# A GNN kernel: the seats' rows of sweep A and of the last layer through two row buffers instead of one

## The chip, the cores and the metric

The kernel runs on one core of one Trainium2 chip. The metric is the device time of one launch in microseconds (us), as the median of several runs. Besides, one execution was recorded by the hardware profiler; every row below is from that execution.

## The reference, cut to what matters

There are 100,000 nodes with 64 features each, and 50,000 edges with their own 64 features, sorted by destination. Four layers are added to `x` one after the other, each on the normalised rows `h = max(layernorm(x), 0)`:

```python
h = jnp.maximum(_layernorm(x, axis=-1), 0.0)
x = x + _L0_gnn_ref(h, edge_index, W3, b3, W4, b4)      # two graph convolutions: sweeps A and B
h = jnp.maximum(_layernorm(x, axis=-1), 0.0)
x = x + _L1_gnn_ref(h, edge_index, edge_attr_64, W, b, eps)   # edge features: sweep C
h = jnp.maximum(_layernorm(x, axis=-1), 0.0)
x = x + _L2_gnn_ref(h, attn_w, temp, src, dst)          # 8 attention steps: layer D
h = jnp.maximum(_layernorm(x, axis=-1), 0.0)
x = x + _L3_gnn_ref(h, src, dst)                        # 10 propagation steps: layer E, the last
```

A step of a layer sums, for each destination, rows gathered from its sources. In `_L0_gnn_ref` the rows are scaled by `dinv`, the inverse root of the degree; in `_L3_gnn_ref` the result of the 10 steps is mixed as `out = out + w[step + 1] * h`, beginning with `w[0] * feat`.

## The kernel before, in words

**Seats and chunks.** Each edge has a seat: partition `p`, column `j`, with 392 columns on 128 partitions. The columns are worked on in `NCH = 28` chunks of `CH = 14`. One chunk of rows is a tile of 128 x 14 x 64 floats, 448 KB. `X` holds the state of the destination at each seat in SBUF, with two more columns (`FC` and the next) for the segments that reach over partitions; these two columns are the "tail" below.

**Tables.** For each sweep a table in HBM (`tab_a` to `tab_e`) holds the rows that are gathered: first those of all nodes, then from row N those of the seats. The nodes' part is written in the dense stage, the first third of the run, in which each tile passes through two row buffers in turn: `row_ac = [rowsA, rowsC]` and `row_be = [rowsB, rowsE]`. The seats' part is written by a pass over the chunks just ahead of each sweep, or within the sweep before.

**The two passes that the change touches.** For sweep A and for layer E nothing is swept while the seats' rows are made, so each has a pass of its own, of 28 iterations.

- VectorE (DVE): wait until the row buffer's last store has landed (`stored["a"]`, `stored["e"]`), then `norm`: 14 `bn_stats` (L1253), a few short operations on the statistics, `sem_inc(var_ready)`, the centred rows `xm` (L1265), wait for the square root of ScalarE, the reciprocal (L1267), the scaled rows into the row buffer (L1269). Pass A then scales them by `dinv` (L1292), pass E adds them to `X` (L1366). Then `sem_inc(rows_ready)` (L1368 in pass E). Pass A first copies the chunk of `dinv` (L1710). Pass A is stage_a with `rowsA` at L1708 to L1714, pass E is stage_e with `rowsE` at L2072 to L2076.
- ScalarE (ACT): `root` (the square root, L735), then `store_rows` (L764): wait for `rows_ready`, issue one DMA of the whole chunk to the table.
- After the 28 chunks comes the tail of two columns, in the same row buffer, and its first column is scattered to the table by GpSimd (POOL) in `front_rows` (L450). Only then, and when all stores have landed, does POOL begin the gathers of the sweep.

**What runs beside them.** In pass A, POOL works off `attr_rows`: for each of 28 chunks it gathers 14 columns of the edge features (L446) into `G` and stores them to `attr` in two halves (L570). POOL comes to `front_rows(tab_a, ...)` after the last of these. In pass E, POOL has nothing to do: the attention steps are over, and the last layer's first gather needs `tab_e`. SyncE (SP) waits on `stored["a"]` (L412) and `f_stored` (L414) before it loads the chunks of `tab_a` for sweep A.

**Order.** Every engine runs its program in order, with loops written out by hand; there is no planner. A register (`Reached`) holds the value of a semaphore that an engine waits for next. `fresh()` clears `dve_step`, on which DVE waits for its own earlier results, once in each loop iteration.

Of the kernel before, what the change touches and what calls it, by code (L numbers as in the profile page):

```python
# [3 lines left out]
def _build(nc, x, src, dst, edge_attr, W3, b3, W4, b4, W1, b1, eps, attn_w, temp, out):  # L4
# [22 lines left out]
    FC = COLS  # L27
    XC = COLS + 2
# [19 lines left out]
    with ctx:  # L48
# [3 lines left out]
        def sem(name):  # L52
            return ctx.enter_context(nc.semaphore(name))
# [4 lines left out]
        tab_a = dram("tab_a", [N + EP, D])  # L58
# [3 lines left out]
        tab_e = dram("tab_e", [N + REG, D])  # L62
# [11 lines left out]
        X = sb("X", [P, XC, D])  # L74
# [16 lines left out]
        dinv = sb("dinv", [P, XC])  # L91
# [40 lines left out]
        mixb = sb("mixb", [P, K3 + 1])  # L132
# [24 lines left out]
        rowsA = sb("rowsA", [P, CH, D])  # L157
# [50 lines left out]
        row_ac = [rowsA, rowsC]  # L208
        row_be = [rowsB, rowsE]
# [13 lines left out]
        dve_step = sem("dve_step")  # L223
# [37 lines left out]
        x_free = [sem("x_free0"), sem("x_free1")]  # L261
        out_stored = [sem("out_stored0"), sem("out_stored1")]
        rows_ready = sem("rows_ready")
        stored = {k: sem(f"stored_{k}") for k in "abcde"}
        dense_stored = {k: [sem(f"dense_{k}0"), sem(f"dense_{k}1")] for k in "abcde"}
        var_ready = sem("var_ready")
        sd_ready = sem("sd_ready")
# [12 lines left out]
        f_rows = sem("f_rows")  # L280
# [24 lines left out]
        FIRST = 1  # L305
# [15 lines left out]
        def wide(t, n=D):  # L321

            return t.unsqueeze(2).to_broadcast([t.shape[0], t.shape[1], n])
# [16 lines left out]
        def _(sp):  # L340
# [62 lines left out]
            sp.wait_ge(widest_stored, 16)  # L403
            sp.dma_start(WB[:, 2:7], widest.rearrange("a o -> o a").to_broadcast([P, 5])).then_inc(widest_loaded, 16)
            r_fs = Reached(sp, "sp_fs")
            r_st = {k: Reached(sp, f"sp_stored_{k}", FIRST) for k in "abc"}
            for k, t in (("a", tab_a), ("b", tab_b), ("c", tab_c)):
                if k == "c":
                    sp.wait_ge(attr_stored[0], 16 * NCH)
                    sp.wait_ge(attr_stored[1], 16 * NCH)  # L410
                sp.wait_ge(stored[k], r_st[k].more(16 * NCH))
                sp.sem_inc(sp_waited, 1)  # L412
                sp.wait_ge(f_stored, r_fs.more(16))
                sp.sem_inc(sp_waited, 1)  # L414
                with sp.Fori(0, NCH // 2) as i:
                    for s in (0, 1):
                        c = 2 * i + s
                        sp.wait_ge(used[s], r_used[s].reg)
                        sp.sem_inc(sp_waited, 1)
                        r_used[s].skip(1)  # L420
                        sp.dma_start(own[:, s, :, :], seats(t, N, c)).then_inc(own_loaded[s], 16)
                        if k == "c":
                            sp.dma_start(ea[:, s, :, :], seats(attr, 0, c)).then_inc(ea_loaded[s], 16)

        @block.gpsimd
        def _(pool):
# [203 lines left out]
                pool.wait_ge(f_stored, r_fs.more(16))  # L630
                pool.sem_inc(pool_waited, 1)

            r_stored = {k: Reached(pool, f"pool_stored_{k}", FIRST) for k in "abcde"}
            front_rows(tab_a, F_TAB_W, fown[:, 0, :])
            pool.wait_ge(stored["a"], r_stored["a"].more(16 * NCH))
            pool.sem_inc(pool_waited, 1)
            pool.wait_ge(dense_stored["a"][0], FIRST + 16 * NT // 2)
            pool.wait_ge(dense_stored["a"][1], FIRST + 16 * NT // 2)
# [34 lines left out]
                    pool.wait_ge(step_done, r_sd.more(1))  # L673
                    pool.sem_inc(pool_waited, 1)
            front_rows(tab_e, F_TAB_W, rowsE[:, 0, :])
            pool.wait_ge(stored["e"], r_stored["e"].more(16 * NCH))
            pool.sem_inc(pool_waited, 1)
            pool.wait_ge(dense_stored["e"][0], FIRST + 16 * NT // 2)
            pool.wait_ge(dense_stored["e"][1], FIRST + 16 * NT // 2)
# [45 lines left out]
        def _(act):  # L725
# [48 lines left out]
            for s in (0, 1):  # L774
                act.sem_inc(raw_stored[s], FIRST)
                act.sem_inc(out_stored[s], FIRST)
                for k in "abcde":
                    act.sem_inc(dense_stored[k][s], FIRST)
            for k in "abcde":
                act.sem_inc(stored[k], FIRST)  # L780

            r_be = [Reached(act, f"act_be{s}", FIRST) for s in (0, 1)]
# [76 lines left out]
            act.wait_ge(var_ready, r_var.more(1))  # L859
            nc.scalar.activation(tmpB[:, :], snE[:, :], ACT.Sqrt).then_inc(sd_ready, 1)  # L860

            with act.Fori(0, NCH) as c:
                root(CH)
                store_rows(seats(tab_a, N, c), rowsA[:, :, :], stored["a"])
            root(2)

            def raw_and_hidden(c, s, before=None):
# [55 lines left out]
            with act.Fori(0, NCH) as c:  # L923
                root(CH)
                store_rows(seats(tab_e, N, c), rowsE[:, :, :], stored["e"])
            root(2)

            def step_e(table, first, k):
# [160 lines left out]
        def _(dve):  # L1089
# [5 lines left out]
            r_stored = {k: Reached(dve, f"dve_st_{k}", FIRST) for k in "abcde"}  # L1095
# [12 lines left out]
            def nth():  # L1108

                steps[0] += 1  # L1110
                return steps[0]
# [160 lines left out]
            def xcols(c):  # L1272
                return X[:, ds(c * CH, CH), :]
# [16 lines left out]
            def stage_a(xr, dv, R, ready):  # L1290
                norm(xr, rowsA[:, 0:R, :], R)
                v.tensor_tensor(rowsA[:, 0:R, :], rowsA[:, 0:R, :], wide(dv), ALU.mult).then_inc(dve_step, 1)  # L1292
                dve.wait_ge(dve_step, nth())
                dve.sem_inc(ready, 1)

# [64 lines left out]
                attention_row(rowsD[:, 0:R, :], xr, R)  # L1360
                dve.sem_inc(ready, 1)

            def stage_e(xr, R, ready):

                norm(xr, rowsE[:, 0:R, :], R)
                v.scalar_tensor_tensor(xr, rowsE[:, 0:R, :], mixb[:, 0:1], xr, ALU.mult, ALU.add).then_inc(dve_step, 1)  # L1366
                dve.wait_ge(dve_step, nth())
                dve.sem_inc(ready, 1)  # L1368

# [335 lines left out]
            dve.wait_ge(dve_step, nth())  # L1705

            dve.wait_ge(x_gathered, 16 * (COLS + 1))
            with dve.Fori(0, NCH) as c:  # L1708
                fresh()
                v.tensor_copy(chn[:, 0, :], dinv[:, ds(c * CH, CH)]).then_inc(dve_step, 1)  # L1710
                dve.wait_ge(dve_step, nth())
                dve.wait_ge(stored["a"], r_stored["a"].reg)
                r_stored["a"].skip(16)
                stage_a(xcols(c), chn[:, 0, :], CH, rows_ready)  # L1714
            dve.wait_ge(stored["a"], r_stored["a"].reg)
            stage_a(X[:, FC:XC, :], dinv[:, FC:XC], 2, f_rows)
# [352 lines left out]
            with dve.Fori(1, K2 + 1) as k:  # L2069
                fresh()  # L2070
                step_d(k)
            with dve.Fori(0, NCH) as c:  # L2072
                fresh()
                dve.wait_ge(stored["e"], r_stored["e"].reg)
                r_stored["e"].skip(16)
                stage_e(xcols(c), CH, rows_ready)  # L2076
            dve.wait_ge(stored["e"], r_stored["e"].reg)
            v.tensor_copy(idxC[:, :], idxA[:, :]).then_inc(dve_step, 1)
            dve.wait_ge(dve_step, nth())
            stage_e(X[:, FC:XC, :], 2, f_ready)  # L2080
            dve.wait_ge(f_stored, r_fs.more(16))
            begin()

# [81 lines left out]
```

## Time and profile before

| | us |
|---|---|
| median of 3 runs | 9849.85 |
| lowest and highest run | 9848.82 and 9856.18 |
| profiled execution, its own time | 9845.43 |
| its span | 9843.8 |
| DVE busy | 5536.8 (56%) |
| POOL busy | 6361.7 (65%) |
| ACT busy | 593.6 (6%) |
| PE busy (matmul) | 1625.2 (17%) |

The span is the time from the first to the last recorded instruction. An engine's share of busy time is a mean over stages that differ: dense stage, sweeps A to C, attention steps, last layer. The end of the run is set by whichever engine is last in each stage, so a pass is judged by its own stretch: pass A lies between about 3426 and 3693 us, pass E between about 7402 and 7664 us.

### The profile page before, as it was taken

The page shows a single profiled execution, that of the slowest core. Times are in us where ns is not written, and L with a number is a line of the kernel's source. Part 1 is how long each engine was busy: PE and PEld are TensorE (multiplying, and loading weights), DVE is VectorE, ACT ScalarE, POOL GpSimd, SP SyncE. Part 2 cuts the span into 40 slices and gives each one's busy share as a digit, 9 for nine tenths or more (in the row PEclk, how much of TensorE's full clock was granted, in tenths as well). Part 3 has the DMA queues.
Part 4 walks back from the last instruction along what each step waited for, and adds up shares of the span by engine and source line. Part 5 has one row for each costly group of instructions (what it writes and reads, how often), then busy time and mean ns, then how long its engine had stood idle before and what let it go on. Part 6 is the DMA issues. An engine that isn't in the chain of part 4 may idle for free.

```text
span 9843.8 us, 60633 instructions
## 1 busy us (share of the span) xinstructions
PE 1625.2 (17%) x7434; PEld 1157.5 (12%) x7434; DVE 5536.8 (56%) x16716; ACT 593.6 (6%) x1219; POOL 6361.7 (65%) x6415
## 2 busy tenths in 40 slices
PE   5634231210244302540012200000000000000000
PEld 1223131110233201430011100000000000000000
DVE  6769484683999861436678845545446443333310
ACT  0011010000111100110000000000001000000000
POOL 6767755527477777767767577666640677777777
PEclk9855555555555555555555555555555555555555
DMA  0022120100234432333333322242221121333320
GB/s 10 11 80 95 49 78 31 52 28 0 71 114 124 115 88 67 91 84 90 91 93 100 86 45 50 43 42 39 37 27 45 43 47 40 44 42 39 35 26 19
DMA packets 588778, 568.96 MB, mean 58 GB/s; under 512 B 420588, under 2 KB 426657, under 8 KB 588624
## 3 DMA queue, kind: packets, MB, share of 16 engines
q0 software_dynamic: 193184, 160.50, 12.3%
q10 hardware_dynamic: 368192, 328.20, 10.0%
q1 hardware_dynamic: 27346, 79.76, 2.4%
q14 instruction: 51, 0.42, 0.0%
q8 instruction: 5, 0.08, 0.0%
HBM read 214.35 MB, written 357.51 MB: 58 GB/s over the span
## 4 chain that ended last, share of the span: by engine, by line
POOL 44%; issue 24%; DVE 19%; DMA 11%; POOLq 1%; DVEq 1%; PE 0%; SPq 0%; ACTq 0%; ACT 0%
POOL G L446 23%; POOL look L446 5%; DVE G L1740 5%; POOL X L446 4%; POOL pair L446 4%; POOL seatmap L450 4%; POOL out L450 3%; DMA G<-in_edge_attr,idxs 1%; DVE st L1253 1%; DMA G<-tab_d,idxs 1%; DMA alt_d<-G 1%; DMA G<-alt_d,idxs 1%; DMA tab_e<-rowsE 1%; DVE xm L1278 1%; DVE G L1989 1%
## 5 line engine op out<-in xcount | busy, mean ns | idle before, releaser
L446 POOL DMA_INDIRECT G<-tab_e,idxs x644 | 681.7, 1058 | 230.3 <-issue 188.8
L446 POOL DMA_INDIRECT G<-tab_d,idxs x616 | 640.2, 1039 | 221.2 <-issue 176.6
L446 POOL DMA_INDIRECT look<-flagtab,idxs x588 | 614.9, 1046 | 206.8 <-issue 170.2
L2118 DVE TENSOR_TENSOR G<-G,chn 128x896 f32<-128x896 f32 x76 | 83.2, 1095 | 938.8 <-DMA G<-tab_e,idxs 548.0
L446 POOL DMA_INDIRECT X<-in_x,dst_gat x392 | 421.1, 1074 | 249.1 <-issue 125.8
L446 POOL DMA_INDIRECT G<-alt_e,idxs x420 | 444.7, 1059 | 154.7 <-issue 127.6
L446 POOL DMA_INDIRECT G<-tab_c,idxs x392 | 441.9, 1127 | 142.9 <-issue 117.7
L974 PE MATMUL TR<-w4T,shared 128*128 128x64 f32 x2356 | 488.7, 402 | 190.2 <-ACT shared L753 190.2
L446 POOL DMA_INDIRECT G<-tab_b,idxs x392 | 419.2, 1069 | 141.1 <-issue 113.5
L446 POOL DMA_INDIRECT pair<-lookup,idxs x392 | 418.5, 1068 | 140.3 <-issue 116.5
L974 PEld LDWEIGHTS TR<-w4T,shared 128*128 128x128 f32 x2356 | 475.4, 312 | 283.5 <-issue 283.5
L446 POOL DMA_INDIRECT G<-in_edge_attr,idxs x392 | 413.1, 1054 | 140.9 <-issue 129.8
L446 POOL DMA_INDIRECT G<-alt_d,idxs x392 | 408.2, 1041 | 140.6 <-issue 113.7
L450 POOL DMA_INDIRECT seatmap<-vals,idxs x392 | 399.5, 1019 | 140.8 <-issue 116.5
L446 POOL DMA_INDIRECT G<-tab_a,idxs x392 | 395.4, 1009 | 141.4 <-issue 110.8
L991 PE MATMUL HP<-ident,tcar 128*64 128x128 f32 (+1 forms) x21 | 8.7, 416 | 2694.5 <-DVEq L1189 2694.5
L1253 DVE BATCH_NORM_STATS2 st<-xin 128x6 f32<-128x64 f32 x3136 | 419.1, 210 | 57.9 <-DVE rowsC L1269 17.1
L984 PE MATMUL TR<-w1Te,hT 64*128 64x64 f32 x1568 | 182.1, 420 | 1188.5 <-ACT hT L743 1188.5
L1964 DVE RECIPROCAL sm<-G 128x14 f32<-128x14 f32 x72 | 17.4, 242 | 617.8 <-DMA G<-tab_d,idxs 361.3
L1740 DVE SCALAR_TENSOR_TENSOR G<-G,chn 128x64 f32<-128x64 f32 x1092 | 311.6, 285 | 39.1
L966 PE MATMUL HP<-hT,w3T 64*128 64x512 f32 (+1 forms) x676 | 282.0, 982 | 235.3 <-ACT hT L743 235.3
L991 PEld LDWEIGHTS HP<-ident,tcar 128*64 128x64 f32 (+1 forms) x21 | 3.2, 150 | 2698.6 <-issue 2698.6
(465 smaller groups left out, 7530.5 us busy)
## 6 DMA issues: line engine op xcount, KB each, us to landing
raw<-G ACTq DMA_DIRECT2D x84, 448.0 KB, 3.6
tab_d<-rowsD ACTq DMA_DIRECT2D x56, 469.0 KB, 2.6
tab_d<-G ACTq DMA_DIRECT2D x56, 469.0 KB, 2.8
xin<-in_x SPq DMA_DIRECT2D x56, 448.0 KB, 5.6
tab_a<-rowsA ACTq DMA_DIRECT2D x56, 448.0 KB, 2.5
tab_b<-rowsB ACTq DMA_DIRECT2D x56, 448.0 KB, 2.8
out<-shared ACTq DMA_DIRECT2D x56, 448.0 KB, 5.6
tab_c<-rowsC ACTq DMA_DIRECT2D x56, 448.0 KB, 2.6
```

What stands on the lines that cost most here:

```text
L446: pool.indirect_dma_start(to, None, table, bass.IndirectOffsetOnAxis(ap=index, axis=0), bounds_check=bound, oob_is_err=False).then_inc(s, 16)
L450: pool.indirect_dma_start(table, bass.IndirectOffsetOnAxis(ap=index, axis=0), frm, None, bounds_check=bound, oob_is_err=False).then_inc(s, 16)
L966: last = nc.tensor.matmul(HP[:, 2 * h + g, 0:(b - a) * P], w3T[h * D:(h + 1) * D, :], hT[h * D:(h + 1) * D, a:b, :].rearrange("p a b -> p ...
L974: last = nc.tensor.matmul(T[:, r * D:(r + 1) * D], U[:, r % 2, r // 2, :], w4T[:, :], start=True, stop=True)
L984: last = nc.tensor.matmul(T[:, at:at + D], hT[h * D:(h + 1) * D, r // 2, :], w[h * D:(h + 1) * D, :], start=True, stop=True)
L991: nc.tensor.transpose(to, frm, ident[0:n, 0:n]).then_inc(turned, 1)
L1253: last = v.bn_stats(st[:, r, :], xr[:, r, :])
L1278: v.tensor_tensor(xm[:, 0:R, :], to[:, :, 0:D], flat_rows(attn[:, k * D:(k + 1) * D], R), ALU.mult).then_inc(dve_step, 1)
L1740: v.scalar_tensor_tensor(G[:, s, j, 0:W], before, go[:, j:j + 1], G[:, s, j, 0:W], ALU.mult, ALU.add).then_inc(dve_step, 1)
L1964: v.reciprocal(r1, g[:, :, D + 2]).then_inc(dve_step, 1)
L1989: v.tensor_tensor(g, g, wide(p, AW), ALU.mult).then_inc(dve_step, 1)
L2118: v.tensor_tensor(g, g, wide(chn[:, 1, :]), ALU.mult).then_inc(dve_step, 1)
```

## The change

Both passes now go two chunks to an iteration, `s = 0` and `s = 1`, and 14 iterations. Chunk `2i + s` goes through `row_ac[s]` (pass A: `rowsA`, `rowsC`) or `row_be[s]` (pass E: `rowsB`, `rowsE`). Each buffer has a store semaphore of its own, `seats_stored[k][s]`, in place of the one `stored[k]`; whoever waited for all 28 stores now waits on both, with 14 each. The tail of pass A stays in `rowsA` and waits on the stores of buffer 0; the tail of pass E stays in `rowsE` and waits on those of buffer 1.

```diff
-        stored = {k: sem(f"stored_{k}") for k in "abcde"}
+        stored = {k: sem(f"stored_{k}") for k in "bcd"}
+        seats_stored = {k: [sem(f"seats_{k}0"), sem(f"seats_{k}1")] for k in "ae"}
...
-                sp.wait_ge(stored[k], r_st[k].more(16 * NCH))
+                if k == "a":
+                    sp.wait_ge(seats_stored["a"][0], FIRST + 16 * NCH // 2)
+                    sp.wait_ge(seats_stored["a"][1], FIRST + 16 * NCH // 2)
+                else:
+                    sp.wait_ge(stored[k], r_st[k].more(16 * NCH))
...
-            pool.wait_ge(stored["a"], r_stored["a"].more(16 * NCH))
+            pool.wait_ge(seats_stored["a"][0], FIRST + 16 * NCH // 2)
+            pool.wait_ge(seats_stored["a"][1], FIRST + 16 * NCH // 2)
... (the same for "e")
-            with act.Fori(0, NCH) as c:
-                root(CH)
-                store_rows(seats(tab_a, N, c), rowsA[:, :, :], stored["a"])
+            with act.Fori(0, NCH // 2) as i:
+                for s in (0, 1):
+                    root(CH)
+                    store_rows(seats(tab_a, N, 2 * i + s), row_ac[s][:, :, :], seats_stored["a"][s])
... (the same for "e", with row_be)
-            with dve.Fori(0, NCH) as c:
+            with dve.Fori(0, NCH // 2) as i:
                 fresh()
-                v.tensor_copy(chn[:, 0, :], dinv[:, ds(c * CH, CH)]).then_inc(dve_step, 1)
-                dve.wait_ge(dve_step, nth())
-                dve.wait_ge(stored["a"], r_stored["a"].reg)
-                r_stored["a"].skip(16)
-                stage_a(xcols(c), chn[:, 0, :], CH, rows_ready)
-            dve.wait_ge(stored["a"], r_stored["a"].reg)
-            stage_a(X[:, FC:XC, :], dinv[:, FC:XC], 2, f_rows)
+                for s in (0, 1):
+                    c = 2 * i + s
+                    v.tensor_copy(chn[:, 0, :], dinv[:, ds(c * CH, CH)]).then_inc(dve_step, 1)
+                    dve.wait_ge(dve_step, nth())
+                    dve.wait_ge(seats_stored["a"][s], r_seats["a"][s].reg)
+                    r_seats["a"][s].skip(16)
+                    stage_a(row_ac[s][:, :, :], xcols(c), chn[:, 0, :], CH, rows_ready)
+            dve.wait_ge(seats_stored["a"][0], r_seats["a"][0].reg)
+            stage_a(rowsA[:, 0:2, :], X[:, FC:XC, :], dinv[:, FC:XC], 2, f_rows)
...
-            with dve.Fori(0, NCH) as c:
+            with dve.Fori(0, NCH // 2) as i:
                 fresh()
-                dve.wait_ge(stored["e"], r_stored["e"].reg)
-                r_stored["e"].skip(16)
-                stage_e(xcols(c), CH, rows_ready)
-            dve.wait_ge(stored["e"], r_stored["e"].reg)
+                for s in (0, 1):
+                    dve.wait_ge(seats_stored["e"][s], r_seats["e"][s].reg)
+                    r_seats["e"][s].skip(16)
+                    stage_e(row_be[s][:, :, :], xcols(2 * i + s), CH, rows_ready)
+            dve.wait_ge(seats_stored["e"][1], r_seats["e"][1].reg)
             v.tensor_copy(idxC[:, :], idxA[:, :]).then_inc(dve_step, 1)
             dve.wait_ge(dve_step, nth())
-            stage_e(X[:, FC:XC, :], 2, f_ready)
+            stage_e(rowsE[:, 0:2, :], X[:, FC:XC, :], 2, f_ready)
```

`stage_a` and `stage_e` take the buffer as their first argument, and their operations stay the same ones.

## Rows read from the trace of the kernel before

**Rows 1.** The page, its chain that ended last, by engine.

```profile
POOL 44%; issue 24%; DVE 19%; DMA 11%; POOLq 1%; DVEq 1%; PE 0%; SPq 0%; ACTq 0%; ACT 0%
```

**Rows 2.** POOL's waits, 7664 to 9500: line, releaser, us, times, longest us.

```profile
POOL tab_e L450 <- DVEq L1368: 268.2, 1, 268.2
```

**Rows 3.** DVE's waits in pass E, 7401.6 to 7664.

```profile
DVE st L1253 <- DMA tab_e<-rowsE: 76.7, 27, 2.9
DVE idxC L2078 <- DMA tab_e<-rowsE: 2.7, 1, 2.7
```

**Rows 4.** Timeline, first chunks of pass E: start, duration, what, [idle before <- releaser].

```profile
7402.22 1.87 DVE L1253 BATCH_NORM_STATS2 st<-X 128x6 f32 x14 [0.68 <-DVE eidx L1923]
...
7407.46 1.15 DVE L1366 SCALAR_TENSOR_TENSOR X<-rowsE,mixb,X 128x896 f32 x1
7408.86 0.34 ACTq L764 DMA_DIRECT2D tab_e<-rowsE  x1
7409.53 1.28 ACT L735 ACT_TABLE_LOAD   x1 [4.23 <-DVEq L1368]
7411.46 1.87 DVE L1253 BATCH_NORM_STATS2 st<-X 128x6 f32 x14 [2.85 <-DMA tab_e<-rowsE]
...
7414.25 0.31 ACT L735 ACTIVATE lnw<-lnw,lneps 128x14 f32<-128x14 f32 x1 [3.43 <-DVEq L1264]
```

**Rows 5.** Chain that ended last, a piece of pass E: start, us, what.

```profile
7408.86 2.44 DMA tab_e<-rowsE
```

**Rows 6.** Timeline of DVE in layer E: between chunks, at a loop's end and inside its body.

```profile
7798.39 0.17 DVE L2113 COPY chn<-cont 128x14 f32 x1 [0.78 <-DVE X L2124]
...
7817.78 0.17 DVE L2113 COPY chn<-cont 128x14 f32 x1 [0.26 <-DVE X L2124]
```

**Rows 7.** DVE's waits in pass A, 3426 to 3693.

```profile
DVE st L1253 <- DMA tab_a<-rowsA: 59.4, 28, 3.0
DVE chn L1710 <- DVE rowsA L1292: 18.0, 27, 0.7
```

**Rows 8.** DVE's waits in the dense stage, 500 to 3380.

```profile
DVE st L1253 <- DVE rowsC L1269: 16.6, 20, 0.9
DVE st L1253 <- DVE rowsA L1269: 10.3, 27, 0.4
```

**Rows 9.** One line of the code: DVE's waits on semaphores within stage_a, min/median/max ns.

```profile
L1294 DVEq EVENT_SEMAPHORE  x29: 21/21/21, 3433.2 to 3692.3; - x29
```

**Rows 10.** Timeline of ACT in layer D: table loads of two successive loop iterations.

```profile
5714.30 1.28 ACT L772 ACT_TABLE_LOAD   x1 [7.39 <-issue]
5753.39 1.28 ACT L772 ACT_TABLE_LOAD   x1 [7.35 <-issue]
```

**Rows 11.** Timeline, end of pass A.

```profile
3692.36 0.23 DVE L1717 COPY fown<-rowsA 128x128 f32<-128x128 f32 x1
```

**Rows 12.** Timeline of POOL: heads of attr chunks in and after pass A, then front_rows.

```profile
3453.47 0.21 POOL L557 COPY idxs<-eidx 128x14 int32 x1
...
3688.70 0.21 POOL L557 COPY idxs<-eidx 128x14 int32 x1
...
3711.19 0.21 POOL L557 COPY idxs<-eidx 128x14 int32 x1
...
3778.86 0.21 POOL L557 COPY idxs<-eidx 128x14 int32 x1
3798.19 0.98 POOL L570 DMA_DIRECT2D attr<-G  x1
3804.98 1.07 POOL L450 DMA_INDIRECT tab_a<-fown,fidx  x1 [3.50 <-issue]
```

**Rows 13.** SP's waits, 3300 to 3900.

```profile
SPq L412 <- DMA tab_a<-rowsA: 265.7, 1, 265.7
SPq L414 <- DMA tab_a<-fown,fidx: 117.2, 1, 117.2
```

**Rows 14.** The tile attr: time from issue to landing of its DMAs.

```profile
DMA to landing us min/median/max: 3.1/3.1/6.9
```

More of the change, by code:

```diff
@@ L405, in _ @@
             r_fs = Reached(sp, "sp_fs")
-            r_st = {k: Reached(sp, f"sp_stored_{k}", FIRST) for k in "abc"}
+            r_st = {k: Reached(sp, f"sp_stored_{k}", FIRST) for k in "bc"}
             for k, t in (("a", tab_a), ("b", tab_b), ("c", tab_c)):
@@ L631, in front_rows @@
                 pool.sem_inc(pool_waited, 1)
-            r_stored = {k: Reached(pool, f"pool_stored_{k}", FIRST) for k in "abcde"}
+            r_stored = {k: Reached(pool, f"pool_stored_{k}", FIRST) for k in "bcd"}
             front_rows(tab_a, F_TAB_W, fown[:, 0, :])
-            pool.wait_ge(stored["a"], r_stored["a"].more(16 * NCH))
+            pool.wait_ge(seats_stored["a"][0], FIRST + 16 * NCH // 2)
+            pool.wait_ge(seats_stored["a"][1], FIRST + 16 * NCH // 2)
             pool.sem_inc(pool_waited, 1)
@@ L675, in _ @@
             front_rows(tab_e, F_TAB_W, rowsE[:, 0, :])
-            pool.wait_ge(stored["e"], r_stored["e"].more(16 * NCH))
+            pool.wait_ge(seats_stored["e"][0], FIRST + 16 * NCH // 2)
+            pool.wait_ge(seats_stored["e"][1], FIRST + 16 * NCH // 2)
             pool.sem_inc(pool_waited, 1)
@@ L778, in _ @@
                     act.sem_inc(dense_stored[k][s], FIRST)
-            for k in "abcde":
+                for k in "ae":
+                    act.sem_inc(seats_stored[k][s], FIRST)
+            for k in "bcd":
                 act.sem_inc(stored[k], FIRST)
@@ L922, in _ @@
                 step_d(tab_d, N, 2 * n + 2)
-            with act.Fori(0, NCH) as c:
-                root(CH)
-                store_rows(seats(tab_e, N, c), rowsE[:, :, :], stored["e"])
+            with act.Fori(0, NCH // 2) as i:
+                for s in (0, 1):
+                    root(CH)
+                    store_rows(seats(tab_e, N, 2 * i + s), row_be[s][:, :, :], seats_stored["e"][s])
             root(2)
@@ L1094, in _ @@
             r_turned = Reached(dve, "dve_turned")
-            r_stored = {k: Reached(dve, f"dve_st_{k}", FIRST) for k in "abcde"}
+            r_stored = {k: Reached(dve, f"dve_st_{k}", FIRST) for k in "bcd"}
+            r_seats = {k: [Reached(dve, f"dve_seats_{k}{s}", FIRST) for s in (0, 1)] for k in "ae"}
             r_gat = [Reached(dve, f"dve_gat{s}") for s in (0, 1)]
@@ L1288, in attention_row, with stage_a @@
                 dve.wait_ge(dve_step, nth())
-            def stage_a(xr, dv, R, ready):
-                norm(xr, rowsA[:, 0:R, :], R)
-                v.tensor_tensor(rowsA[:, 0:R, :], rowsA[:, 0:R, :], wide(dv), ALU.mult).then_inc(dve_step, 1)
+            def stage_a(to, xr, dv, R, ready):
+                norm(xr, to, R)
+                v.tensor_tensor(to, to, wide(dv), ALU.mult).then_inc(dve_step, 1)
                 dve.wait_ge(dve_step, nth())
@@ L1361, in stage_d, with stage_e @@
                 dve.sem_inc(ready, 1)
-            def stage_e(xr, R, ready):
-                norm(xr, rowsE[:, 0:R, :], R)
-                v.scalar_tensor_tensor(xr, rowsE[:, 0:R, :], mixb[:, 0:1], xr, ALU.mult, ALU.add).then_inc(dve_step, 1)
+            def stage_e(to, xr, R, ready):
+                norm(xr, to, R)
+                v.scalar_tensor_tensor(xr, to, mixb[:, 0:1], xr, ALU.mult, ALU.add).then_inc(dve_step, 1)
                 dve.wait_ge(dve_step, nth())
@@ L2071, in _ @@
                 step_d(k)
-            with dve.Fori(0, NCH) as c:
+            with dve.Fori(0, NCH // 2) as i:
                 fresh()
-                dve.wait_ge(stored["e"], r_stored["e"].reg)
-                r_stored["e"].skip(16)
-                stage_e(xcols(c), CH, rows_ready)
-            dve.wait_ge(stored["e"], r_stored["e"].reg)
+                for s in (0, 1):
+                    dve.wait_ge(seats_stored["e"][s], r_seats["e"][s].reg)
+                    r_seats["e"][s].skip(16)
+                    stage_e(row_be[s][:, :, :], xcols(2 * i + s), CH, rows_ready)
+            dve.wait_ge(seats_stored["e"][1], r_seats["e"][1].reg)
             v.tensor_copy(idxC[:, :], idxA[:, :]).then_inc(dve_step, 1)
             dve.wait_ge(dve_step, nth())
-            stage_e(X[:, FC:XC, :], 2, f_ready)
+            stage_e(rowsE[:, 0:2, :], X[:, FC:XC, :], 2, f_ready)
             dve.wait_ge(f_stored, r_fs.more(16))
```

## The prediction

> **What bounds the kernel now.** I read the chain that ended last first. POOL has 44% of it, DVE 19%, DMA 11% [rows 1]: mostly the run waits for POOL's gathers, but there are stages in which DVE and a DMA are last. So the two passes have to be looked at one by one, and the question for each is who waits for whom at its end.
>
> Pass E is on the path. POOL sits idle for 268.2 us until DVE's `sem_inc` after the tail (L1368) [rows 2]; the pass with its tail takes the whole of that. Within it DVE waits 27 times, 76.7 us in total, for the store of the chunk before to land [rows 3]: 2.84 us each. The order in a chunk is strict [rows 4]: the last operation on the rows ends at 7407.46 + 1.15 = 7408.61, ACT issues the store at 7408.86, it takes 2.44 us to land [rows 5], and only then, at 7411.46, does the next `bn_stats` start, which doesn't touch the row buffer at all. From the first `bn_stats` to the end of L1366 DVE needs 7408.61 - 7402.22 = 6.39 us, so the period of 9.24 us is 6.39 of work and 2.85 of waiting.
>
> Pass A is not on the path. It looks alike: 59.4 us of waits for the store (28 times, the last of them the tail's), and 18.0 us of gaps at the loop's end [rows 7]. But its tail is over at 3692.6 [rows 11], while POOL is still at the edge features: the head of its last chunk is at 3778.86, the store of its first half is issued at 3798.19, and `front_rows` of `tab_a` comes at 3804.98 [rows 12]. DVE's result lies ready for 112 us. SP says the same: 117.2 us in its wait for that scatter, after the wait for pass A [rows 13].
>
> **The change part by part.**
>
> *Pass E, the waits removed.* Chunk c now waits for the store of chunk c-2. That store is issued 0.25 us after the end of its chunk and lands 2.44 us later, at +2.69 us; DVE asks for the buffer one chunk and two gaps later, 6.39 + 0.3 + 0.75 = +7.4 us. A landing would have to take 7.1 us to be felt. So all 27 waits go: -76.7 us.
>
> *Pass E, what was hidden beneath these waits.* Between two chunks DVE still has to signal `rows_ready`, add to a register, look at a semaphore, compute the address of the next chunk, and at the loop's end branch and clear `dve_step`. This has been free under the DMA, and now shows. The trace has the same pair of gaps in layer E's loop, also two chunks to a body: 0.78 us at the loop's end and 0.26 us inside the body [rows 6]. Pass A's own loop end is 18.0 / 27 = 0.67 us [rows 7]. In the dense stage, two waits and two register additions ahead of the `bn_stats` give 10.3 / 27 = 0.38 inside the body and 16.6 / 20 = 0.83, longest 0.9, at the loop's end [rows 8]. One more wait than in rows 6 is 0.02 us [rows 9]. I take 0.30 inside the body (bounds 0.26 and 0.38) and 0.75 at the loop's end (bounds 0.67 and 0.9), near rows 6 since that is the closest code. There are 14 steps from s = 0 to s = 1 and 13 back: 14 x 0.30 + 13 x 0.75 = 4.2 + 9.75 = 13.95 us. With the bounds, 14 x 0.26 + 13 x 0.67 = 12.3 and 14 x 0.38 + 13 x 0.9 = 17.0.
>
> *Pass E, next in line: ACT.* Its square root must be ready. After the store's issue ACT loads its function table from 7409.53 to 7410.81, that is 2.20 us after the end of L1366 [rows 4]. The square root itself is called for 7414.25 - 7411.46 = 2.79 us after `bn_stats` starts. With gaps of 0.30 and 0.75 that is at +3.1 and +3.5, so 0.9 and 1.3 us are left: nothing is late. If that cover were too short it would cost the difference per chunk. Besides, a loop with two chunks to a body needs one load in each iteration, as in layer D, where they are 39.1 us apart [rows 10], so I expect 13 or 14 loads instead of 27.
>
> The Trainium skill counts more for this load: in "ScalarE: Activation LUTs", section "What ACT_TABLE_LOAD costs", about 1283 ns and then a drain of about 1380 ns, 2.66 us in all. The first figure is that of rows 4; a drain no row here shows, since no activation follows a load closely. By that page ACT would be free at +3.58 us: 0.04 us late after a loop's end, 0.5 us late inside the body if there is a load there too, so an estimate of 0.5 us in total with one load per iteration, 7 us with one per chunk.
>
> *Pass E, the tail.* The last chunk used `rowsE`, the tail does too, and it waits for that store: the 2.7 us of L2078 [rows 3] stay. POOL's and SP's second wait are on semaphores that are long reached, 0.02 us each [rows 9].
>
> Pass E: -76.7 + 13.95 = -62.7 us, bounds -64.4 and -59.7. POOL's first gather of layer E starts by so much earlier, and after that nothing is changed: POOL bounds the ten steps as before.
>
> *Pass A.* The same arithmetic makes it some 60 us shorter, and all of it goes into waiting: SP waits for `front_rows` for some 177 us instead of 117, POOL doesn't look. 0 us. The tail of pass A has no wait any more, since buffer 0 is free by then; 0 as well.
>
> *Pass A, beside POOL.* Here may be a small effect of unknown sign. From 3453.47 to 3688.70 POOL needs 235.23 / 10 = 23.52 us a chunk, from 3711.19 to 3778.86 only 67.67 / 3 = 22.56 [rows 12]. So pass A costs POOL, which is on the path, 0.96 us a chunk, some 11 us over its 266 us. If this is tied to the work of DVE and the 28 stores, which stay the same in number, nothing changes. If it is tied to the time in which both run, a pass shorter by 60 us gives 0.96 x 60 / 23.5 = 2.5 us back. If denser stores collide more, the most I allow is that the excess doubles: 11 us lost. I take 0, between the two and near the first, as the work is what collides.
>
> **Sum.** -62.7 us. The profiled execution took 9845.43, its span 9843.8, so I expect 9782.7 and 9781.1 there. It stood 4.4 below the median of the runs; from the median, 9849.85 - 62.7 = 9787.1. I predict 9787.
>
> **The rivals.**
>
> 1. *Pass A, denser, slows POOL.* For: the 0.96 us a chunk above; the stores then come every 7 us instead of every 9.3. Against: no more bytes or operations, and POOL has only some nine chunks under pass A instead of eleven. 9787 + 11 = 9798.
>
> 2. *A new wait in pass E takes the place of the old*, on ACT's square root or in a store that lands late beside the next chunk's operations. For: DVE and the store now overlap fully, which in this pass has not been. Against: the slack of 0.9 us and more worked out above, and the dense stage, which overlaps in the same way with gaps of 0.4 and 0.8 [rows 8]. If half of each wait stayed, 27 x 1.42 = 38.3 with the gaps within it, the gain is 38 us: 9812.
>
> 3. *The pass isn't what holds POOL.* If something else would end its wait just as late, the time stays 9850. For: only that sweep A shows how it goes, with 112 us of cover [rows 11, 12]. Against: in pass E POOL has no work, and its wait ends with DVE's signal [rows 2].
>
> 4. *Slower: the doubled loop bodies.* A body twice as long might have to be fetched again at each jump back. The longest landing of a DMA in the attr stores is 6.9 us [rows 14]; 13 such stalls in pass E are 90 us, less the 62.7 gained, 9877. It decides from 62.7 / 13 = 4.8 us a jump; at the 2.44 us of a store the result would still be 31 us faster. Against: the dense loop's body has some 196 DVE operations, pass E's would have 46, and the dense loop turns back in 0.83 us, 0.9 at the most [rows 8]. The Trainium skill has the mechanism ("Runtime: NRT & Kernel Launch", section "Instruction fetch mechanics"): a taken branch outside the two-page window has to fetch its target first. Rows 8 show no trace of it at four times the length.
>
> **How the numbers follow.** Forecast 0.85; rival 1 0.06; rival 2 0.06; rival 3 0.02; rival 4 0.01. The forecast's own bounds are 9785.5 (gaps at their lowest) to 9790.1; with 2.5 us back from pass A 9783, with a part of rival 1 about 9795. The runs before lay between 9848.8 and 9856.2, and the profiled one at 9845.4, so the level itself moves by 4 to 6 us either way. The range is 9777 to 9801, which takes in rival 1. About 0.2%, 20 us, is what a measurement of this kernel can tell from no change. Forecast, rival 1 and rival 2 are all faster by more than that: 0.97. Same 0.02, slower 0.01.
>
> **What would show it.** In the changed profile: no wait of `bn_stats` for a DMA in pass E, but gaps of about 0.3 and 0.75 us in turn; a pair of chunks in 2 x 6.39 + 1.05 = 13.8 us; POOL's wait at L450 down from 268.2 to about 205 us; the tail's wait still 2.7; ACT's table loads in pass E 13 or 14. Pass A over near 3632 us and SP's wait at L414's place near 177, with POOL's scatter of `fown` within 3 us of 3805. I would be wrong if POOL's wait in pass E fell by clearly less than 60 us, if that scatter moved by more than 5 us, or if the layers after pass E took longer than before.

## The result, and the profile after

| | before | after |
|---|---|---|
| median (8 runs each, same chip) | 9848.61 | 9814.67 |
| lowest and highest run | 9839.02 and 9856.18 | 9806.85 and 9832.76 |
| profiled execution, its own time | 9845.43 | 9815.84 |
| its span | 9843.8 | 9814.2 |
| pass E: last scatter of layer D to first of layer E | 269.3 | 209.2 |
| eight attention steps | 1737.0 | 1747.9 |
| ten steps of the last layer | 1823.7 | 1837.6 |

The ratio is 0.9968, with a 95% interval of 0.9957 to 0.9979: 33.9 us faster, where 62.7 were forecast, and outside the range given. The stages in the table are measured between POOL's `fidx` scatters, as in [rows 12].

Pass E does what it should. These are DVE's waits in it, the view of [rows 3] (line and tile, releaser, us in total, times, longest us):

```profile
DVE st L1265 <- DVE X L1378: 14.9, 27, 0.9
DVE idxC L2093 <- DMA tab_e<-rowsE: 2.7, 1, 2.7
```

The 76.7 us of waiting for a store are gone. In their place are 14.9 us of gaps, where 13.95 were forecast, and the tail's 2.7 stay. In the timeline of DVE, as in [rows 4 and 6], the two gaps follow each other (start, duration, what, idle before):

```profile
7424.21 1.15 DVE L1378 SCALAR_TENSOR_TENSOR X<-rowsB,mixb,X 128x896 f32 x1
7425.67 1.87 DVE L1265 BATCH_NORM_STATS2 st<-X 128x6 f32 x14 [0.31 <-DVE X L1378]
...
7430.92 1.15 DVE L1378 SCALAR_TENSOR_TENSOR X<-rowsE,mixb,X 128x896 f32 x1
7432.94 1.95 DVE L1265 BATCH_NORM_STATS2 st<-X 128x6 f32 x14 [0.86 <-DVE X L1378]
...
7438.27 1.15 DVE L1378 SCALAR_TENSOR_TENSOR X<-rowsB,mixb,X 128x896 f32 x1
```

A pair of chunks takes 7438.27 - 7424.21 = 14.06 us; 13.8 were forecast. The third line holds a detail for later: the 14 `bn_stats` of `s = 0` take 1.95 us, those of `s = 1` 1.87. ACT is on time. Its groups in pass E show 13 table loads, where the kernel before had 27, and its timeline shows the square root called 2.86 us after the start of the `bn_stats` at 7432.94, the load long over:

```profile
L742 ACT ACT_TABLE_LOAD x13 | 16.7, 1283 | 54.9 <-DVEq L1380 54.9
```
```profile
7433.00 1.28 ACT L742 ACT_TABLE_LOAD   x1 [4.24 <-DVEq L1380]
7435.80 0.31 ACT L742 ACTIVATE lnw<-lnw,lneps 128x14 f32<-128x14 f32 x1 [1.52 <-DVEq L1276]
```

Pass A does what was forecast too. SP's waits, against [rows 13], and two tiles (`fown` and `tab_a`), against [rows 11 and 12]:

```profile
SPq L417 <- DMA tab_a<-rowsC: 209.6, 1, 209.6
SPq L419 <- DMA tab_a<-fown,fidx: 178.0, 1, 178.0
```
```profile
L1731 DVE COPY fown<-rowsA x1: 227/227/227, 3635.6 to 3635.6; 128x128 f32<-128x128 f32 x1
L455 POOL DMA_INDIRECT tab_a<-fown,fidx x1: 1072/1072/1072, 3811.4 to 3811.4; - x1
```

Pass A is over 56.8 us earlier, and POOL's scatter comes not earlier but 6.4 us later. That delay is there before pass A begins: the first `attr` store is issued at 3159.8 (3153.2 before), the last at 3807.1 (3800.5), 647.3 us apart both times.

So the rest was lost elsewhere, and POOL's waits say where. Before, from 5650 us to the end, as [rows 2]:

```profile
POOL tab_d L450 <- DVEq L2055: 61.3, 4, 16.7
POOL alt_d L450 <- DVEq L2055: 57.0, 4, 16.7
```

After, the same stretch:

```profile
POOL tab_d L455 <- DVEq L2069: 67.5, 4, 18.6
POOL alt_d L455 <- DVEq L2069: 62.0, 4, 18.6
POOL tab_e L455 <- DVEq L1380: 208.1, 1, 208.1
POOL tab_e L455 <- DVEq L2146: 6.0, 3, 2.0
POOL alt_e L455 <- DVEq L2146: 5.2, 3, 2.0
```

POOL's wait for pass E is 60.1 us shorter (268.2). But it waits 129.5 us for DVE's tail of the attention steps, where it was 118.3: 11.2 us, and these steps are 10.9 us longer. In the last layer there are 11.2 us of waits for the tail which were not there at all. DVE, which [rows 1] had as second, has become later in layers that the diff doesn't touch. The sum over the span, from the scatters: +6.4 to `tab_a`, -0.9 to `tab_d`, +10.9, -60.1, +13.9, and 0.2 behind that make -29.6.

Why DVE is later can be seen in the narrow steps. Each step loops over 14 pairs of chunks with `If(i * (2 * CH) < wide_to)`, and where the widths are small, up to 13 of the 14 bodies are skipped. The line of this loop on DVE's sequencer (the part that reads the instructions and takes the branches) in the eighth of the last layer's ten steps, before and after (count, min/median/max ns, first and last start):

```profile
L2107 DVEq ALU_OP  x14: 40/40/40, 9336.4 to 9343.4; - x14
```
```profile
L2122 DVEq ALU_OP  x14: 40/40/40, 9302.7 to 9312.0; - x14
```

13 skipped iterations take 7.0 us before (0.54 each) and 9.3 after (0.72 each), with the same instructions of the same durations. The two branches of an iteration share the loss: from the branch that turns back to the next instruction it is 0.19 us before and 0.32 after, from the branch over the body 0.20 and 0.26. ACT skips the same iterations in 5.8 us in both. No engine's busy time shows the loss, and the wait view after calls this idle time of DVE "remote". At the end of that step DVE is late by that (timelines, before and then after):

```profile
9344.35 0.41 DVE L1752 TENSOR_TENSOR_SCAN TF<-allcT,HP 64x128 f32<-64x128 f32 x1 [8.07 <-DMA FR<-tab_e,fidx]
...
9348.11 0.98 POOL L450 DMA_INDIRECT tab_e<-FR,fidx  x1 [0.30 <-issue]
```
```profile
9312.93 0.41 DVE L1766 TENSOR_TENSOR_SCAN TF<-allcT,HP 64x128 f32<-64x128 f32 x1 [10.41 <-remote]
...
9315.68 1.16 POOL L455 DMA_INDIRECT tab_e<-FR,fidx  x1 [2.00 <-DVEq L2146]
```

My theory was: the bodies of pass A and pass E, written out twice, are 43 and 40 instructions longer on DVE, and push the loops of layers D and E along by 45 and 85, where the jumps of a skipped iteration are slower. The rival theories were: the doubled bodies or the second buffer slow DVE in another way (semaphores, registers), or the layers' times move from one execution to the next.

### The profile page after: what moved, and what is told of

It reads as the page before. It is cut to its first block, busy times and chain, and to the rows that moved or that the text cites. A ratio compares the mean times of both kernels' runs of the same rounds, so it can differ in the third digit from the quotient of the medians.

```text
span 9814.2 us, 60449 instructions
## 1 busy us (share of the span) xinstructions
PE 1619.4 (17%) x7434; PEld 1151.8 (12%) x7434; DVE 5535.4 (56%) x16716; ACT 575.9 (6%) x1205; POOL 6363.7 (65%) x6415
## 4 chain that ended last, share of the span: by engine, by line
POOL 45%; issue 24%; DVE 19%; DMA 10%; POOLq 1%; DVEq 1%; PE 0%; SPq 0%; ACTq 0%; ACT 0%
POOL G L451 24%; POOL look L451 6%; DVE G L1754 5%; POOL X L451 4%; POOL pair L451 4%; POOL seatmap L455 4%; POOL out L455 3%; DMA G<-in_edge_attr,idxs 1%; DVE st L1265 1%; DMA G<-tab_d,idxs 1%; DMA alt_d<-G 1%; DMA G<-alt_d,idxs 1%; DVE G L2003 1%; DVE xm L1290 1%; DVE rowsD L1293 1%
## 5 line engine op out<-in xcount | busy, mean ns | idle before, releaser
L455 POOL DMA_INDIRECT out<-X,dst_out x266 | 260.0, 977 | 88.6 <-issue 86.3
```

Of the source, the lines that this page charges most:

```text
L455: pool.indirect_dma_start(table, bass.IndirectOffsetOnAxis(ap=index, axis=0), frm, None, bounds_check=bound, oob_is_err=False).then_inc(s, 16)
```

## The experiments

All were timed in five rounds, against the kernel before on the same chip, in three sets of four. The sets ran on three chips. The one of the second behaves as the one above. On the other two DVE begins pass A 235 to 504 us later, and the runs of the kernel before lie 200 and 122 us apart, so that the total can't tell 25 us, and the verdict rests on stretches of the trace. Two measures are used throughout: us per skipped iteration on DVE (last attention step / last step of layer E), and POOL's two waits for the tail in layer D, added up as above. The length of a whole layer scatters more: with the same place of the loops, layer D took 1776.3 and 1765.2 us on the first of the slow chips.

| kernel | ratio (95%) | skipped iteration | POOL's waits, D | layer D | pass E | layer E |
|---|---|---|---|---|---|---|
| before (profile above) | | 0.54 / 0.54 | 118.3 | 1737.0 | 269.3 | 1823.7 |
| after (profile above) | 0.9968 | 0.69 / 0.72 | 129.5 | 1747.9 | 209.2 | 1837.6 |
| slots_two_buffers | 0.9865 (0.9825 to 0.9904) | 0.54 / 0.54 | 118.1 | 1776.3 | 207.8 | 1839.0 |
| slots_across_before | 1.0026 (0.9996 to 1.0056) | 0.71 / 0.69 | 130.6 | 1782.1 | 272.3 | 1843.8 |
| slots_within_before | 1.0016 (0.9978 to 1.0055) | 0.54 / 0.54 | 118.0 | 1765.2 | 269.3 | 1841.8 |
| doubled_one_buffer | 1.0002 (0.9973 to 1.0032) | 0.69 / 0.72 | 129.2 | 1773.7 | 270.1 | 1846.1 |
| changed_again | 0.9969 (0.9957 to 0.9980) | 0.69 / 0.73 | 129.4 | 1758.0 | 209.2 | 1845.5 |
| slots_again | 0.9945 (0.9931 to 0.9958) | 0.54 / 0.54 | 118.1 | 1744.1 | 207.8 | 1836.0 |
| pass_a_only | 1.0006 (0.9997 to 1.0015) | 0.54 / 0.54 | 118.2 | 1744.9 | 269.3 | 1835.4 |
| trip_counts | 0.9899 (0.9884 to 0.9914) | none | 77.1 | 1702.5 | 207.9 | 1836.4 |
| across_again | 1.0016 (0.9994 to 1.0037) | 0.71 / 0.69 | 130.6 | 1759.1 | 272.3 | 1847.6 |
| within_again | 1.0008 (0.9981 to 1.0036) | 0.54 / 0.54 | 118.2 | 1749.0 | 269.3 | 1832.0 |
| doubled_again | 1.0011 (0.9982 to 1.0040) | 0.69 / 0.72 | 129.2 | 1760.2 | 270.2 | 1846.5 |
| pass_a_again | 0.9933 (0.9907 to 0.9958) | 0.54 / 0.54 | 118.0 | 1748.2 | 269.3 | 1836.5 |

**The place of the loops alone.** The loop constructor can pad the program so that the loop's first instruction comes at a given place of a block of 256. `slots_two_buffers` and `slots_again` are the changed kernel with the outer loops over the steps of layers D and E at place 0. They have 176 and 103 instructions on DVE, so that each lies within one block of 256. `slots_within_before` and `within_again` are the kernel before with place 0. `slots_across_before` and `across_again` are the same with place 200: the inner loops, 100 and 61 instructions long, then begin at 213 and 221 and are cut at 256. No operation differs.

```diff
-            with dve.Fori(1, K3 + 1) as k:
+            with nc.Fori(1, K3 + 1, engines=OrderedEngineSet([dve.engine]), head_slot={dve.engine: 0}) as k:
```

> The changed kernel, and VectorE's two step loops (attention steps and last layer's steps) are loaded with their heads at slot 0 of an instruction fetch block, so that each inner loop with its skipped body lies within one block. Nothing else differs. Theory P (placement): the 25 us that the attention steps and the last layer's steps lost came from VectorE's skipped iterations, 0.54 us each before and 0.69 to 0.72 after, because a jump over the body now crosses a block boundary. Then a skipped iteration takes 0.54 us again, POOL's scatters of tab_d (first to last) are 1737 us apart as before instead of 1748, the last layer's steps take 1827 us instead of 1841, and the time falls from 9814.7 to about 9790. Theory S (state or sharing: something that runs denser, or the added semaphores and registers, slows the later steps): placement changes nothing, 9815.

> The kernel before, with the heads of VectorE's two step loops at slot 200 of a fetch block, so that the inner loops (which start at slots 213 and 221) reach over the boundary at 256. No double buffering. Theory P: skipped iterations take about 0.7 us instead of 0.54, the attention steps lose some 11 us and the last layer's steps some 14, and the kernel before becomes about 25 us slower, 9873. Theory S: no difference, 9849.

> The kernel before, with the heads of VectorE's two step loops at slot 0 of a fetch block. Theory P: its loops already lay within a block, so the time stays 9849 within 5 us, and a skipped iteration 0.54 us. If it gets faster by 10 us or more, the boundary is not what tells the two kernels apart. Theory S: 9849 too.

The skipped iteration follows the place: 0.54 at place 0, in the old kernel and in the new one, and 0.69 to 0.71 at place 200, which only the old one was given. (In one step of `slots_within_before` a stretch of 10 us has instructions of the sequencer of up to 0.7 us, and the mean there is 1.05; the other steps of that run have 0.54.) POOL's waits in layer D follow it too, 118 against 130.6, and, where bodies are skipped at all, depend on nothing else: over all sets they are 118.0 to 118.3 in seven traces and 129.2 to 130.6 in six, with nothing between. The last three attention steps, some 80 us each and with 39 skipped iterations, part the same traces: together they take 236.1 to 238.3 us in the seven and 241.8 to 244.6 in the six. The totals of this set tell nothing on 25 us, and the whole of layer D, for which 1737 was expected of `slots_two_buffers`, took 1776.3. That the ratio of `slots_two_buffers` is far better than the theory says has another cause, taken up below.

**The doubled bodies without a second buffer.** The kernel before with both passes written out two chunks to an iteration, still through one row buffer and one semaphore each (`doubled_one_buffer`, `doubled_again`).

```diff
-            with dve.Fori(0, NCH) as c:
+            with dve.Fori(0, NCH // 2) as i:
                 fresh()
-                dve.wait_ge(stored["e"], r_stored["e"].reg)
...
+                for s in (0, 1):
+                    dve.wait_ge(stored["e"], r_stored["e"].reg)
```

> The kernel before with the bodies of both passes doubled (two chunks to an iteration, as in the change), but one row buffer and one store semaphore each. VectorE's program has the length of the changed one, to two instructions. Theory P: no gain in pass E, whose waits stay (POOL's wait for it 268 us), and the loss of the shifted loops in full, so slower than before by 20 to 27 us, about 9873. Theory S, with the denser passes as its cause: 9849, since nothing runs denser.

0.69 and 0.72, as after. So the loss comes with the length of the program, not with buffers or semaphores. Pass E stays at 270, so the gain is the second buffer's alone.

**Where the blocks end.** The places 0 and 200 can't tell a block of 256 instructions from one of 128, since the inner loops lie between two multiples of 128 at place 0 as well, and are cut by one at place 200. But DVE's sequencer shows ends that straight code passes, as 0.05 to 0.12 us more between two instructions, where the engine's own work doesn't hide it. Counted from the head of layer D's step loop: at place 0 (`within_again`) it needs 0.21 us from instruction 127 to 128, at place 200 (`across_again`) 0.10. At place 200 (`slots_across_before`) the extra time comes from 183 to 184, which is at 384 (0.21 for 0.12). `doubled_again` has it from 79 to 80 (0.20 for 0.08), within the inner loop, and from 207 to 208 (0.14 for 0.10 in the first iteration of pass E): 128 apart. So the ends lie at multiples of 128. The program comes in pieces of that kind too: each of the 52 transfers of the instruction queue has 8,192 bytes.

```profile
q14 instruction: 52, 0.43, 0.0%
```

In the changed kernel an end lies in the `bn_stats` of pass E, from 205 to 206; it is what makes 1.95 us of 1.87 there, and 2.21 in the first iteration, and a transfer of q14 begins 0.7 us after that. One multiple of 128 further down and one further up are within the inner loops of layers D (13 to 112) and E (316 to 376). With ends 256 apart, neither would be cut. In the kernel before, with 45 instructions fewer ahead of layer D, the same count puts both loops between two ends.

**Both sides on a chip with quiet totals.**

> The changed kernel as it is, beside the others of this group. Both theories: 0.9966 of the kernel before. In its trace pass E takes 209 us of POOL's waiting, the last three attention steps (scatter to scatter) sum to 242 us, the last seven steps of the last layer to 353, and a skipped iteration of VectorE's takes 0.69 and 0.72 us.

> The changed kernel with the heads of VectorE's two step loops at slot 0 of a fetch block, once more. Theory P: 0.9940 of the kernel before (0.9935 to 0.9950), some 25 us less than the changed kernel of this group; last three attention steps 238 us, last seven steps of the last layer 347. Theory S: as the changed kernel.

`changed_again` gives the result once more (-31.4 us; -33.9 the first time). The last three attention steps take 243.0 and 237.3 us in the two; the 353 and 347 us that were expected for seven steps of layer E fit its last five (356.0 and 346.8). `slots_again` is 55.5 us faster than before and 24.1 faster than `changed_again`; the two intervals just touch, but the traces give the same difference by stages: 13.9 in layer D, 1.4 in pass E, 9.5 in layer E, 24.8 in all. No run of one lies among those of the other (9817.0 to 9823.3, and 9834.5 to 9849.1). POOL's waits of `slots_again` from 7300 us hold no wait for the tail of layer E; the scatters to `tab_e` (and those to `alt_e`, likewise) go ahead as soon as POOL comes to them:

```profile
POOL tab_e L456 <- DVEq L1381: 206.8, 1, 206.8
...
POOL tab_e L456 <- issue: 1.5, 5, 0.3
```

**Pass A alone.** `slots_again` with pass E as it was before; only pass A has two buffers.

```diff
-                for s in (0, 1):
-                    dve.wait_ge(seats_stored["e"][s], r_seats["e"][s].reg)
-                    r_seats["e"][s].skip(16)
-                    stage_e(row_be[s][:, :, :], xcols(2 * i + s), CH, rows_ready)
+                dve.wait_ge(stored["e"], r_stored["e"].reg)
+                r_stored["e"].skip(16)
+                stage_e(rowsE[:, :, :], xcols(c), CH, rows_ready)
```

> Only pass A uses two buffers in turn; pass E is as before (one chunk to an iteration, one buffer). Heads of VectorE's two step loops at slot 0. If pass A is hidden and does nothing to POOL beside it: 1.0000 of the kernel before (within 0.0006), pass A ends some 60 us earlier, POOL's scatter of fown does not move. If its denser stores cost POOL time: 1.0005 to 1.0012, and a chunk of edge features under pass A takes over 24.2 us of POOL's time instead of 23.5.

9881.97 against 9875.02, not told from 0. The pass's tail lies at 3637.6, POOL's scatter at 3823.4 (3822.2 and 3823.3 in the two kernels above): 186 us of cover. On this chip pass A gains nothing. Whether it costs something stays open: both signs that were named for a price are there. The ratio is 1.0006, and POOL's chunks of edge features under pass A take (3613.63 - 3439.86) / 7 = 24.82 us, over the 24.2 named. The other chunks vary by more than that, from 22.5 to 27.1 us, and the ratio's interval holds 1. On the third chip, below, POOL's first to last `attr` store take 661.7 us beside two buffers (`pass_a_again`) and 655.2 beside one (`within_again`).

**No skipped iterations at all.** `slots_again` with the inner loops of DVE, ACT and POOL over only as many pairs as the step is wide.

```diff
-                with dve.Fori(0, NCH // 2) as i:
-                    with dve.If(i * (2 * CH) < wide_to):
+                with dve.Fori(0, (wide_to + (2 * CH - 1)) // (2 * CH)) as i:
+                    if True:
```

> The changed kernel with slots at 0, and on VectorE, ScalarE and POOL the inner loops of the steps run only as often as the step is wide (a loop bound in a register) instead of 14 times with the body skipped. No skipped iteration is left, on any engine. Theory P says that skipped iterations of VectorE are on the path in the attention steps' tails: 76 of them at 0.54 us, 41 us, go there, and in the last layer, where POOL's own skips lie ahead of its scatters, 102 of POOL's at an estimated 0.4 us. So 0.985 to 0.991 of the kernel before; last three attention steps about 215 us instead of 238. If skipped iterations were not on the path, no difference to the kernel with slots at 0.

This is the fastest kernel: 9777.22 against 9875.02, 97.8 us less than before, 42.3 less than `slots_again`. POOL's waits in layer D, `slots_again` and then `trip_counts`:

```profile
POOL tab_d L456 <- DVEq L2070: 61.2, 4, 16.6
POOL alt_d L456 <- DVEq L2070: 56.9, 4, 16.7
```
```profile
POOL alt_d L456 <- DVEq L2070: 38.8, 4, 9.9
POOL tab_d L456 <- DVEq L2070: 38.3, 4, 9.6
```

41.0 us less, and the layer is 41.6 shorter. The edit takes the skips from three engines at once; that it is DVE's that count is argued from the size, since 76 skipped iterations at 0.54 us are 41.0. Layer E stays at 1836.4 (1836.0), where I had expected a gain from POOL's 102 skips, and it isn't there. The profile before shows why: from 9312.8 to 9318.7 POOL's sequencer skips, and POOL itself works through gathers that were issued earlier, with 0.30 us between them as at other times. And DVE, with quick skips, is ready before POOL asks.

**Once more on a third chip.**

> The kernel before with the heads of VectorE's step loops at slot 200 of a fetch block, once more, since the first time the chip's dense stage was so much slower and so scattered that 25 us could not be told. Theory P: 1.0020 to 1.0028 of the kernel before; last three attention steps 242 to 244 us, last seven steps of the last layer 353. Theory S: 1.0000.

> The kernel before with those heads at slot 0, once more. Theory P: 1.0000 of the kernel before, within 0.0007; last three attention steps 236 to 238 us, last seven steps 345 to 348. It is also what pass_a_again is to be compared with.

> Both passes with doubled bodies and one row buffer each, once more. Theory P: 1.0018 to 1.0028 of the kernel before, from nothing but VectorE's longer program ahead of the step loops. Theory S: 1.0000.

> Pass A alone with two buffers, slots at 0, next to the same kernel without it (within_again). Hidden without a price: the two within 5 us of each other, POOL's 28 chunks of edge features take the same time in both. Denser stores at a price: this one 6 to 11 us longer, and the difference lies in the chunks of edge features under pass A.

Within the traces, `across_again` takes 10.1 us longer than `within_again` in layer D, 3.0 in pass E and 15.6 in layer E: 28.7 in all. `doubled_again` has 11.2, 0.9 and 14.5. The total ratios can't tell any of this from 1, nor `doubled_again` from the 1.0018 to 1.0028 expected. The 3.0 us of pass E have the same source as the rest: with the loop at place 200, that pass has an end in its `bn_stats` (1.97 us for 1.87, and 2.25 in the first chunk).

The surprise is `pass_a_again`, the same kernel as `pass_a_only`: 66 us faster than before. The tiles `attr` and `fown` with the scatter in `within_again`, which has one buffer:

```profile
L571 POOL DMA_DIRECT2D attr<-G x56: 959/973/1011, 3226.3 to 3881.5; - x56
```
```profile
L1718 DVE COPY fown<-rowsA x1: 227/227/227, 3956.2 to 3956.2; 128x128 f32<-128x128 f32 x1
L451 POOL DMA_INDIRECT tab_a<-fown,fidx x1: 1072/1072/1072, 3957.5 to 3957.5; - x1
```

Pass A begins at 3692.8 here, not at 3426, and its tail ends 75 us after POOL's last `attr` store. POOL waits for it, and the wait is of the same kind as in pass E. SP's waits of `pass_a_again` say how the cover of [rows 13], 117.2 us, has gone:

```profile
SPq L418 <- DMA tab_a<-rowsC: 209.2, 1, 209.2
...
SPq L420 <- DMA tab_a<-fown,fidx: 3.4, 1, 3.4
```

The pass itself is 263.5 us long with one buffer (`within_again`) and 206.9 with two, so that on this chip it is worth up to 56 us; the ratio's interval, 42 to 94 us, holds that. The two traces can't show the gain at POOL's scatter (3957.5 and 3960.3), since the second's pass began 59 us later. It also explains `slots_two_buffers` on the first of the slow chips: POOL's wait for pass A there was 157.0 us, 211.4 in `slots_within_before`, and of the 123 us gained 61.5 are pass E's and some 54 pass A's.

## Why the prediction was wrong

- **Pass E**: right. 27 waits gone, gaps of 0.30 and 0.82 us (0.31 and 0.86 the first time; 0.30 and 0.75 forecast), 14.9 us of them in all, the tail's wait and ACT's loads as said. 60.1 us gained for 62.7 forecast, inside the step's own bounds of 59.7 and 64.4. Of the 2.6 us short, 0.95 are the gaps at the loop's end. Another 1.4 are the end of a block within the `bn_stats` of `s = 0`: 13 x 0.08, and 0.34 the first time. With place 0 the gap at the loop's end is the same, 0.83 (0.85 the first time), and it is the `bn_stats` that are back at 1.87 us, which makes that pass 1.4 us shorter. The doubled body, 84 instructions long, holds an end in both, and from its branch back to the next instruction it is 0.32 us, where the body before had 0.20. The line of `slots_again` for the one above at 7432.94:

```profile
7439.38 1.87 DVE L1266 BATCH_NORM_STATS2 st<-X 128x6 f32 x14 [0.85 <-DVE X L1379]
```

- **Pass A, hidden**: right on the chip of the profile: tail at 3635.6 for 3632, SP's wait 178.0 for 177. It isn't so on two other chips, which one profile couldn't show.
- **Pass A beside POOL, rival 1**: nothing in this pair, 647.3 us from the first to the last `attr` store in both. The scatter of `fown` did move by more than the 5 us that were named as a sign of being wrong (6.4), but it was as late before pass A. `pass_a_only` leaves a small price open.
- **Rival 2**: no wait came in the place of the old one. **Rival 3**: POOL's wait ended with the pass.
- **The step that failed**: "after that nothing is changed: POOL bounds the ten steps as before", and the same silence on the eight attention steps. They took 10.9 and 13.9 us longer (layers D and E), 24.8 in all. The term that was put at nothing is DVE's skipped iterations, 0.54 us each before, and 0.69 in layer D and 0.72 in layer E after. In layer D, 76 of them at 0.146 us more are 11.1 us, POOL's waits for the tail grew by 11.2 and the layer by 10.9. In layer E, the last five steps have 9.7 of the 13.9. -60.1 + 24.8 = -35.3, where 33.9 were measured, and 29.6 in the profiled pair, in which the dense stage and the sweeps brought 5.7 the other way.
- **Rival 4** named the doubled bodies, but asked only whether they themselves turn back in time. That rows 8 show a long loop turning back in 0.83 us was a fair answer to that question, and 0.86 was the most that the doubled body took. The one not asked was which other loops the new code pushes along, and the cost of a loop that does almost nothing 13 times, which is nearly all jumps. The trace before had what it takes: DVE's loop line in the narrow steps, 0.54 us per skipped iteration, and 118.3 us of POOL waiting for DVE's tail in layer D, which says that any slowdown there goes straight into the end. The prediction looked at the waits of POOL for pass E and not at the 118.3 us beside them.

The Trainium skill ("Runtime: NRT & Kernel Launch", section "Instruction fetch mechanics") has an engine refill its instructions in blocks of 256 and ties a stall to a taken branch whose target is outside the two blocks it holds. That jumps care for blocks agrees with the runs: 0.54 at place 0, 0.69 to 0.71 at place 200. The size doesn't: here the ends lie 128 instructions apart, and a transfer has 8,192 bytes. Nor does it show that only a target outside both blocks costs, since the inner loop cut by one end lies in two neighbouring blocks, and still each skipped iteration costs 0.15 to 0.19 us more.

What stays open: what that time is spent on. It lies behind the two branches, but the profile's instruction queue has 51 transfers before and 52 after, and none of them falls into the skips at 9302 to 9312, so no fetch from memory is recorded for them. Only two places were tried, so it isn't shown how the cost depends on where in the loop the end falls (0.69 to 0.73 in the cases at hand). And why the dense stage ends later on two chips isn't known.

## What to carry to other kernels

A second row buffer in a pass that alone holds up the next engine gives back the waits for the store less the gaps between chunks that they had hidden (76.7 less 14.9 us here, 60.1 measured), and both can be read in the profile. But code added on an engine moves every loop behind it: before calling later stages unchanged, find the loops there that mostly skip their bodies, and the waits for that engine. Where such waits exist, bound the loop by a trip count (here 42 us, more than the second buffers gave net in the first form), or else fix the loop's place, so that no multiple of 128 instructions falls within it.

## What the runs showed of the hardware

- The same loop, instruction for instruction, costs 0.54 or 0.69 to 0.73 us for each skipped iteration on DVE, by its place in the program alone. In layer E, ACT's skip of the same iterations takes 5.8 / 13 = 0.45 us. Longer code can help as well: in layer D, whose steps are written out twice on ACT, every other step had 0.56 us for each skip on ACT before (0.45 in the rest) and 0.44 after. ACT isn't on the path there, and its place wasn't varied.
- DVE's block ends lie 128 instructions apart: straight code takes 0.05 to 0.12 us more where it passes one (0.34 in the first iteration of the changed pass E), and a loop that is cut by one takes 0.06 to 0.13 us more behind each of its two branches.
- The cost of the skips is visible neither as busy time nor as a wait with a name: the profile puts it down to "remote", or to whatever was released last.
- The same kernel has a median of 9849, 9875, 10148 and 10363 us in the four comparisons. What is on the path differs with it: pass A has 112 us of cover in the first profile and none on two chips, where DVE begins it 235 to 504 us later. In the dense stage of `slots_within_before` DVE has waits that the kernel before didn't have in its profile above:

```profile
DVE xin L1312 <- ACT rowsB L792: 93.3, 12, 17.7
DVE lnw L1257 <- remote: 72.1, 16, 8.9
```
